# A planner with a clock per engine, weight rests on GpSimd, and most row normalisations on ScalarE

## What is computed

```
x = x + attn_a(layernorm(x))    channel attention, 8 heads, with its own RMS norm
x = x + ffn(layernorm(x))       router, 8 experts, hidden 336
x = x + attn_b(layernorm(x))    512 x 512 scores, bands of a sigmoid, softmax, projection
x = x + ffn(layernorm(x))       the same weights again

ffn:    probs = softmax(h @ router_w.T)
        k     = argmax(clip(gelu(h @ actor_w1.T + b1) @ actor_w2.T + b2, -30, 30)) + 1
        out   = sum over e of (probs[e] if rank(e) < k else 0) * (silu(h @ gate_w[e].T) * (h @ up_w[e].T)) @ down_w[e].T
attn_b: s = (q @ k.T) * 8 ** -0.5, times 2, 1.5, 1, 0.3 or 0.1 by the band of sigmoid(s), then softmax
```

## Time and profile before

| | us |
|---|---|
| median of 3 runs (lowest, highest) | 562.09 (560.51, 563.34) |
| the profiled execution | 562.99 |
| its span, first to last instruction | 561.2 |
| PE busy | 508.4 (91%) |
| DVE busy | 368.8 (66%) |
| POOL busy | 279.2 (50%) |
| ACT busy | 239.4 (43%) |
| mean clock granted to PE, share of full | 0.963 |

### The profile page before, as it was taken

How to read it: one execution, slowest core, us unless ns; L and a number is a source line. 1 busy time by engine, 2 the same in 40 slices (tenths; PEclk the granted TensorE clock), 3 DMA queues, 4 the chain that set the end, 5 groups by cost and what they waited for, 6 DMA issues and landing times. The chain is left out here.

```text
span 561.2 us, 6465 instructions
## 1 busy us (share of the span) xinstructions
PE 508.4 (91%) x2134; PEld 359.3 (64%) x2134; DVE 368.8 (66%) x781; ACT 239.4 (43%) x399; POOL 279.2 (50%) x268
## 2 busy tenths in 40 slices
PE   7776487999897988999998999979999999999997
PEld 6754364667564764677655677656776576667664
DVE  3646737366649789678989279894797946274221
ACT  3355232444372264732654424744337452433221
POOL 4111516722875239554465434554455455464753
PEclk9979779999998999899998899998999999999999
DMA  8500000000000000000000000000000000000000
GB/s 254 169 1 1 1 0 2 0 0 1 1 2 0 1 0 1 1 0 2 1 1 0 1 0 2 0 0 2 19 2 0 1 19 1 1 2 19 1 0 19
DMA packets 7917, 7.38 MB, mean 13 GB/s; under 512 B 716, under 2 KB 7756, under 8 KB 7884
## 3 DMA queue, kind: packets, MB, share of 16 engines
q1 hardware_dynamic: 7884, 6.97, 4.0%
HBM read 5.91 MB, written 1.05 MB: 12 GB/s over the span
## 5 line engine op out<-in xcount | busy, mean ns | idle before, releaser
L513 POOL TENSOR_TENSOR t<-t,sbc 128x512 f32<-128x512 f32 x168 | 217.5, 1314 | 126.8 <-DVE t L859 98.3
L859 DVE TENSOR_TENSOR t<-bank,sl 128x512 f32<-128x512 f32 x168 | 114.5, 685 | 134.1 <-PE bank L927 106.0
L616 ACT ACTIVATE sl<-bank 128x512 f32<-128x512 f32 x168 | 100.0, 597 | 181.1 <-PE bank L927 163.5
L1061 PE MATMUL bank<-t,WD 128*128 128x512 f32 x336 | 168.2, 603 | 0.0
L925 PE MATMUL bank<-xhF,WGh 128*128 128x512 f32 x168 | 99.6, 593 | 22.4 <-DVE WUl L743 21.2
L1061 PEld LDWEIGHTS bank<-t,WD 128*128 128x128 f32 x336 | 64.7, 192 | 32.6 <-issue 19.8
L925 PE MATMUL bank<-xhF,WUh 128*128 128x512 f32 x168 | 69.1, 411 | 4.1 <-DVE t L859 4.1
L927 PE MATMUL bank<-xhF,WUl 128*128 128x512 f32 x168 | 68.5, 408 | 0.0
L926 PE MATMUL bank<-xlF,WUh 128*128 128x512 f32 x168 | 68.5, 407 | 0.0
L927 PE MATMUL bank<-xhF,WGl 128*128 128x512 f32 x168 | 68.0, 405 | 0.0
L926 PE MATMUL bank<-xlF,WGh 128*128 128x512 f32 x168 | 67.8, 403 | 0.0
(11 more groups left out here) (176 smaller groups left out, 683.6 us busy)
## 6 DMA issues: line engine op xcount, KB each, us to landing
stage<-in_gate SPq DMA_DIRECT2D x7, 192.0 KB, 5.3
stage<-in_up SPq DMA_DIRECT2D x7, 192.0 KB, 5.6
WD<-in_down SPq DMA_DIRECT2D x7, 192.0 KB, 5.6
X<-in_x SPq DMA_DIRECT2D x4, 256.0 KB, 5.2
out<-X SPq DMA_DIRECT2D x4, 256.0 KB, 2.3
raw<-in_small SPq DMA_DIRECT2D x1, 388.0 KB, 4.4
raw<-in_small SPq DMA_DIRECT2D x1, 192.0 KB, 2.7
rows<-in_row SPq DMA_DIRECT2D x1, 136.0 KB
```

The costliest lines, as they stand in the source:

```text
L513: pool.tensor_tensor(t2[k % NT2][:, :], t2[k % NT2][:, :], sbc[k // CH % 2][:, :], ALU.mult).then_inc(a_done, 1)
L616: act.activation(sl[k % NSL][:, :], bank[k % 2][:, :], ACT.Silu).then_inc(silu_done, 1)
L859: dve.tensor_tensor(t2[k % NT2][:, :], bank[2 + k % 2][:, :], sl[k % NSL][:, :], ALU.mult).then_inc(t2_done, 1)
L1061: pe.matmul(OACC[:, :], WD[:, c, :], t2[k % NT2][:, :], start=(c == 0), stop=(c == CH - 1))\
```

## The change

1. `plan()` is written anew. It has a clock for each engine and a table of what each step takes on each engine in turn (STAGES), the load of an ACT table included. Threads are sorted by a deadline in chunks. At PE's present time it first adds steps of the other engines whose inputs are there and whose engine is not more than so far ahead (2.6, 1.6, 1.5 us), then a PE step whose inputs have been there for 0.5 us, or else a `down` or a chunk.
2. `gu` is two steps, `gate` and `up`; the copy of OACC on ACT is a step of its own, `yc`.
3. The rests of 12 of the 14 weight pieces are made on POOL; pieces 0 and 1 stay on DVE. Pieces 3 and 4 are taken ahead of the first chunk.
4. The `xn` of norms 3 to 15 runs on ACT as x * rstd + (-mean * rstd), scale and bias per row. POOL's part of `stats` gets two more instructions for it. Norms 0 to 2 stay on DVE.

```
+STAGES = dict(
+    stats=(("dve", 1.35), ("pool", 2.0)), xn=(("act", 1.2),), xT=(("pe", .45), ("act", .6)), xl=(("dve", .7),),
...
+    bqk=(("pe", .7), ("act", 1.2)), bqkl=(("pool", 1.4),), bs=(("pe", .7), ("act", .6)), bsp=(("dve", 1.7),),
+    bexp=(("exp", .85),), bv=(("pe", 1.35), ("dve", .7)), bpT=(("pe", .45), ("act", .6)), bo=(("pe", .9),),
...
+    um=(("pool", 1.35),), down=(("pe", .86),), warm=())
+DVE_NORMS = 3
+TABLE = 1.3
+HOP = 0.1
+PE_MARGIN, BANK_MARGIN = 0.5, 0.3
+DVE_AHEAD, ACT_AHEAD, POOL_AHEAD = 2.6, 1.6, 1.5
...
+        for e, cost in stages(s, order):
+            if e in ("exp", "silu"):
+                cost += TABLE * (table[0] != e)
+                table[0] = e
+                e = "act"
...
+            at = max(at + HOP, t[e]) + cost
+            t[e] = at
...
+                    if begins <= gus and at <= now + 0.2 and banks_free(s) <= now \
+                            and max(t[e], at) + min(cost, 1.6) <= now + ahead[e]:
+                        add(s)
...
+        if down_at <= now:
+            add(("down", downs))
+            downs += 1
+        elif can_gu and (gu_at <= now + 1.5 or gu_at <= down_at):
+            add(("gate", gus))
+            add(("up", gus))
+            add(("uk", gus))
+            gus += 1
...
@@ POOL @@
+                    if seq >= DVE_NORMS:
+                        pool.tensor_scalar(nms[seq % 2][:, :], mv[:, :, 0], -1.0, None, ALU.mult)
                     chain(pool.tensor_scalar(rt[:, :], mv[:, :, 1], by, more, ALU.mult, ALU.add))
-                    pool.tensor_tensor(rstd[:, :], rt[:, :], nhalf[:, :], ALU.pow).then_inc(rstd_ready, 1)
+                    r = pool.tensor_tensor(rstd[:, :], rt[:, :], nhalf[:, :], ALU.pow)
+                    if seq >= DVE_NORMS:
+                        chain(r)
+                        r = pool.tensor_tensor(nmrs[seq % 2][:, :], nms[seq % 2][:, :], rstd[:, :], ALU.mult)
+                    r.then_inc(rstd_ready, 1)
...
+                if kind == "wp":
+                    j = s[1]
+                    pool.wait_ge(wh_ready, 2 * (j // 3) + j % 3 + 1)
+                    hi, lo = piece_of(j)
+                    pool.tensor_tensor(lo, stage[j][:, :], hi.bitcast(F32), ALU.subtract).then_inc(wl_pool, 1)
@@ ACT @@
+                if kind == "xn" and norm_no[s[1:]] >= DVE_NORMS:
...
+                    act.wait_ge(rstd_ready, seq + 1)
+                    for i in range(NT):
+                        r = act.activation(xns[seq % 2][:, i, :], X[:, NT * (b % NB) + i, :], ACT.Identity,
+                                           bias=nmrs[seq % 2][:, i:i + 1], scale=rstds[seq % 2][:, i:i + 1])
+                    r.then_inc(xn_act, 1)
@@ DVE @@
-                if kind in ("wp", "wpl") and s[1] % 3 != 2:
+                if kind == "wpl":
@@ PE @@
-                        pe.wait_ge(wl_dve, 2 * (c // WCH) + 2)
+                        pe.wait_ge(wl_pool if c else wl_dve, 2 * (c // WCH) if c else 2)
```

More of the change, by code:

```diff
@@ L107 @@
 FREED_BY = dict(asim="ascale", asT="amax", act="actk")
[L109 to L124, removed]
-def needs(s):
[L130 to L134, removed]
-        return [("y", b - 2), ("ag", b)]
[L136 to L152, removed]
@@ L165, in plan @@
-    pieces = [("wp", j) for j in range(2, NPIECES)]
-    steps, done, order = [], set(), {}
-    free_after = []
[L168 to L184, removed]
+    steps, fin, order = [], {}, {}
@@ L201, in add, with chunk_inputs @@
             free_after.extend([by] * TURNS[s[0]])
[L203 to L214, removed]
+    def chunk_inputs(s):
+        k = s[1]
+        n, c = k // CH, k % CH
+        if s[0] == "up":
+            return [("uk", k - 2)] if k >= 2 else []
+        first = [("xl", "F", n)] if c == 0 else []
+        weights = [(w, 3 * (k // WCH) + i) for w in ("wp", "wpl") for i in range(2)] if k < CH and c % WCH == 0 else []
+        return first + [w for w in weights if w in fin] + ([("gate", k - 2)] if k >= 2 else [])
@@ new lines, in banks_free, with ready_at @@
+    def banks_free(s):
+        if s[0] == "bo" and s[2]:
+            return 0.0
+        ends = [free_after[len(free_after) + i - 3] for i in range(TURNS.get(s[0], 0)) if len(free_after) + i >= 3]
+        return max([fin.get(v, 1e9) for v in ends], default=0.0)
+    def ready_at(s):
+        before = [s[:1 + (s[0] in ("stats", "xn", "xT", "xl"))] + (batch(s) - 1,) + s[2 + (s[0] in ("stats", "xn", "xT", "xl")):]]
+        if s[0] == "wp":
+            before = []
+        if not all(v in fin or batch(v) < 0 for v in inputs(s) + needs(s) + before):
+            return 1e9
+        if s[0] == "xn":
+            i = order[s[1:]]
+            others = [v for v, j in order.items() if j == i - 1]
+            two = [v for v, j in order.items() if j == i - 2]
+            if not all(("xn",) + v in fin for v in others) or not all(("xT",) + v in fin for v in two):
+                return 1e9
+        if s[0] == "stats":
+            two = [v for v, j in order.items() if j == len(order) - 2]
+            if not all(("xn",) + v in fin for v in two):
+                return 1e9
+        return max([fin[v] for v in inputs(s)], default=0.0)
@@ L215, in plan @@
     for s in PRELUDE:
-        assert ready(s), s
+        assert ready_at(s) < 1e8 and banks_free(s) < 1e8, s
         add(s)
[L218 to L223, removed]
-        else:
[L225 to L231, removed]
-                s = th[1][0][1]
-                cost = COST.get(s[0], (0, 0, 0))
-                room = pe + cost[0] + DEBT
-                late = (th[2] < SHIFTS
-                        and (act + cost[1] > room + (cost[1] > 2) * 3 or dve + cost[2] > room))
[L237 to L240, removed]
-                th[1].pop(0)
-                add(s)
-                pe, act, dve = pe + cost[0], act + cost[1], dve + cost[2]
-        if pieces:
-            add(pieces.pop(0))
-        debt = [max(0.0, act - pe), max(0.0, dve - pe)]
@@ L247, in plan @@
-    assert not any(th[1] for th in threads)
-    while downs[0] < last:
-        k += 1
-        products(k, 2)
+    norm = ("stats", "xn", "xT", "xl")
+    f_kinds = [(k,) for k in norm] + [("route",), ("rexp",), ("inner", 0), ("inner", 1), ("rsum",), ("tanh",), ("gelu",),
+                                      ("rrank",), ("act",), ("actk",), ("sbc",)]
+    a_kinds = [(k,) for k in ("stats", "xn", "ag", "xT", "ar", "asim", "ass", "ascale", "asT", "amax", "aexp", "awo",
+                              "am", "am2", "y")]
@@ new lines, in plan, with thread @@
+    b_kinds = [("stats",), ("xn",), ("xT",), ("xl",), ("bqk", 0), ("bqkl", 0), ("bqk", 1), ("bqkl", 1)]
+    for i in range(NT):
+        b_kinds += [("bs", i)] + [("bsp", i, part) for part in range(4)] + [("bexp", i)] + [("bv",)] * (i == 0)
+    b_kinds += [("bpT", j) for j in range(NT)] + [("bo", i) for i in range(NT)] + [("byx",)]
+    def thread(what, b, kinds):
+        all_ = [(k[0], what, b) if k[0] in norm else (k[0], b) + k[1:] for k in kinds]
+        return [s for s in all_ if s not in fin]
@@ new lines, in plan @@
+    threads.sort(key=lambda th: th[0])
+    gus, ums, downs = 0, 0, 0
+    ahead = dict(dve=DVE_AHEAD, act=ACT_AHEAD, pool=POOL_AHEAD)
+    while downs < last:
+        now = t["pe"]
+        more = True
+        while more:
+            more = False
+            for _, begins, th in threads:
+                for s in [v for v in th if STAGES[v[0]][0][0] != "pe"]:
+                    e, cost = STAGES[s[0]][0]
+                    e = "act" if e == "exp" else e
+                    at = ready_at(s)
+                    if begins <= gus and at <= now + 0.2 and banks_free(s) <= now \
+                            and max(t[e], at) + min(cost, 1.6) <= now + ahead[e]:
+                        add(s)
+                        th.remove(s)
+                        more = True
+            if ums < gus and ("sbc", ums // CH) in fin and fin["uk", ums] <= now + 0.2 and t["pool"] <= now + 0.4:
+                add(("um", ums))
+                ums += 1
+                more = True
+        best = None
+        for _, begins, th in threads:
+            for s in [v for v in th if STAGES[v[0]][0][0] == "pe"]:
+                if begins <= gus and ready_at(s) + PE_MARGIN <= now and banks_free(s) + BANK_MARGIN <= now:
+                    best = best or (s, th)
+        if best:
+            add(best[0])
+            best[1].remove(best[0])
+            continue
+        first = [v for v in [("xl", "F", gus // CH)] if gus % CH == 0]
+        weights = [("wp", 3 * (gus // WCH) + i) for i in range(2)] if 2 * WCH > gus >= CH or WCH <= gus < CH else []
+        can_gu = gus < last and all(v in fin for v in first + weights) and (gus < NT2 or downs > gus - NT2)
+        gu_at = max([fin[v] for v in chunk_inputs(("gate", gus)) + chunk_inputs(("up", gus))], default=0.0) if can_gu else 1e9
+        down_at = fin["um", downs] + PE_MARGIN if downs < ums else 1e9
+        if down_at <= now:
[6 more added lines that the diff above has]
```

(12 more changed lines are left out.)

143 lines of the change are left out of this document (101 added, 42 removed).

## The result

The kernel became much slower: 650.66 us in the median of four runs (641.09, 645.43, 655.89, 655.94) against 562.72, with a ratio of 1.142 (95% interval 1.128 to 1.156). The forecast was 528.

A forecast was written before the change was run, and what follows sets the result against it. PE was taken to bound the kernel, by its work, idle time and lower clock. 563.0 - 23.5 (first pass) - 15.3 (rest of the program) + 4 (table loads) = 528 us, range 507 to 549.

The forecast's parts named there:

- its floor: Whole kernel: PE's work at full clock, 490.6 us, plus head and end; time not below 503.0 us.
- The first pass: 28 to 98 us: moving rests and `xn` off DVE, with early pieces, recovers most of 29.5 us lost: -23.5.
- the 6 kept: 28 to 98 us: loss expected to remain, from late `sbc`, closely spaced silus and slower `rsum`; ends 0 and 15.
- The meeting of `rsum` with POOL's pieces: First pass: the `rsum` compare and three more such DVE instructions slow beside POOL's pieces, at most 4 us on DVE.
- The prices of the moved work: A norm on ACT 1.6 us, a rest on POOL 1.05, POOL's two new instructions 0.22 each.
- The table loads: 16 more on ACT, 20.5 us; late silus at six bare exps cost PE 0 to 9.5, taken as +4.
- the longer visit (541): Rival: a table change holds ACT longer than its load, 2.6 us per added bare visit, 13 in all: 541; chance 0.02.
- the term of the rest of the program: 98 to 546 us: the new planned list recovers half of 30.3 us of idle time and clock loss: -15.3.
- My signs of being wrong: Silu waits (L714) past 10 us, `uk` waits over 15, or the clock falling as often in B as before.
- The slower rival: B's runs of chunks without `down`: mask steps on DVE cost 1.2 us per chunk, 52 more, 580 us; chance 0.05.
- break-even of 0.9 us per chunk: In the rival that it becomes slower: the cost per chunk without `down` that eats the 38 us gained.
- The moves: Norms 3 to 15 to ACT take 36.2 us off DVE's 369; rests on POOL cost 12.6 us there.

The follow-up runs named there:

- o1: The kernel before, in its old order, with both moves (13 `xn` on ACT, 12 rests on POOL): 562.23 us, ratio 0.9998.
- o4: The kernel before with the weight pieces earlier in the list, all rests and norms still on DVE: 543.30 us, ratio 0.967.
- f2: The changed kernel, planner inputs still empty, with `down` k only once chunk k+1 is listed, plus one wait behind DVE's reciprocal: 546.15 us, ratio 0.972.
- f4: The changed kernel with the planner constants of f3, but the inputs of `uk`, `um` and `down` left empty: 656.21 us, ratio 1.160.
- f3: The changed kernel with the planner's inputs of `uk`, `um` and `down` filled in and other planner constants: 517.21 us, ratio 0.9205.
- b3: The kernel before with AFTER_POOL changed from 1.6 to -1, so 82 of 168 `down` stand directly behind their own chunk's `um`: 883.65 us, ratio 1.557.
- o5: The kernel before with the early pieces of o4 and both moves (rests on POOL, 13 norms on ACT): 540.38 us, ratio 0.959.

## Why the prediction was wrong

**Right.** What bounds the kernel and its floor: 490.6 us of work and a time of 503.0; the fastest version, with its waits nearly gone, is at 517.2. **The first pass**: a loss of 5.7 us for the 6 kept, `sbc` copied at 56.1 us (52 to 62), pieces ready in time. Its reason was half wrong: I had DVE's load and the norms beside POOL's products as the cause of the 21.2 us; o1 (load gone, wait still 20.7) and o4 (load as it was, wait gone) show that the pieces' place in the list decides. The meeting of `rsum` with POOL's pieces, for which part of the 6 was kept, did not happen: the compare (now L919) took 0.43 us at 38.15, where POOL was idle, so these runs don't show what it would have cost. That the 5.7 matched the 6 is partly luck. **The prices of the moved work**: a norm on ACT 1.64 us (1.6), a rest on POOL 1.02 to 1.09 (1.05), POOL's two new instructions 0.23 and 0.20 in the median (0.22 each), and no drain around a table load (the idle time ahead of 28 of them is 0.5 us in all). Groups by line of the changed kernel:

```profile
L714 ACT ACT_TABLE_LOAD x28 | 35.9, 1283 | 0.5
L618 ACT ACTIVATE xn<-X,nmr,rstd 128x128 f32<-128x128 f32 x52 | 21.4, 484 | 0.9 <-POOL nmr L564 0.8
L596 POOL TENSOR_TENSOR WUl<-stage,WUh 128x384 fp32r<-128x384 f32 x6 | 6.5, 1091 | 5.8 <-ACT WUh L685 5.8
```

and a norm in its ACT timeline:

```profile
63.18 1.64 ACT L618 ACTIVATE xn<-X,nmr,rstd 128x128 f32<-128x128 f32 x4
```

**The table loads**, +4: PE's waits for silu are 4.5 us in all, 0.7 before, and four of the five, 4.3 us, come right behind an exp between two loads, the longest with 1.85 (up to 1.9 forecast). The term held, and the longer visit (541) did not come.

**The step that failed** is the term of the rest of the program: "A list made with a clock per engine from costs close to these rows should place the steps better", and from it "I let half of the loss go: -15.3, with 0 and -30.3 as ends". Both ends were wrong, as no loss was allowed. In its place came, in the profiled execution, 54 us more idle and 39 of the lower clock. I judged the planner by its costs, which are right, and not by its edges: three steps of every chunk had no inputs. I also asked of the list only how many chunks had no `down` behind them, a question about too few products between chunks. The fault was the opposite one, products too close behind their own chunk, and the list's last eight lines show it without any trace. f2 and f4 against f3 settle that it is this: one rule on the distance takes some 96 us back, other constants none. My signs of being wrong could not have caught it either: they named waits for silu and for `uk`, which stayed at 4.5 and nothing, and none for `um`; only the clock's falls spoke.

**The slower rival** (0.05) had the wrong mechanism: mask steps in runs of chunks without `down`. PE's waits for `uk`, 4.1 us before, are gone from its list, and the fastest version has more such chunks (82 for 70) with 2.8 us of these waits. Its price per chunk, 1.2 us without the clock, was also under what a closed round costs, 2.1 of wait and, in b3, 1.5 of clock. (Its break-even of 0.9 us per chunk left out the 4 us of the table loads: 35 us over 43 chunks is 0.8.)

**The moves** were priced by an engine's busy time (36 us off DVE). They were worth nothing in the old order (o1), about 3 us or nothing with early pieces (o5), and 43 in a tight list made for them. What stays open is how much of that 43 a list made for norms on DVE would win back.

## What to carry to other kernels

Before a written-out order is trusted, count for each consumer the engine's work between it and its producer in that same order: a consumer that follows its own producer closes a round over all the engines between them (here PE, DVE and POOL), whatever the planner's clocks say. Check a planner's table of inputs against the program's waits, and its own finish time against a measured span; here 500.8 against 654.1 blind, 505.3 against 515.2 repaired. And relief of an engine that is not the bound is worth only what the order can use of it: nothing in o1, about 3 us or nothing in o5, 43 us in the list that was made for it.

## What the runs showed of the hardware that was not expected

The lower clock added some 70% to the fault's price: 39 us on 54 of idle time in the changed kernel, 125 on 184 in b3. It fell within rounds that have only 2.12 us of idle time each. The same rounds ran at full clock from 600 to 609.6 us and at half from there to 643.7 (after); in b3_at_once the longest stretch at half lasts 54.6 us:

```profile
776.30:830.90 54.60, 37.60 (x67) 20.44 (x66) 5.54 (x8) 4.78 (x8) 10.10 (x8) 0.50 0.00 0
```

What decides between the two levels in such rounds these runs don't show. With the clock at 1.00 throughout, the same 2134 matmuls took 492.4 us, with the fault 547.3 and 633.8.

Four `xn` instructions on DVE take 1.1 us where POOL is idle and 3.6 to 5.1 where it works nearly all the while, while six of POOL's products beside such an `xn` take 7.69 us, 1.28 each, for a mean of 1.31 over all of them: nearly all of the price of that meeting falls on DVE, where the prediction had the two hold each other up.
